# Transposed scores that accumulate key differences in PSUM, with half-height second passes side by side, in a fused attention and FP4 feed-forward kernel

## What is computed

```python
x = x + attn(layernorm(x))          # B, N, DIM = 4, 1024, 128
x = x + ffn(layernorm(x))           # hidden width 352

def attn(x):
    q, k, v = heads(x @ Wq.T), heads(x @ Wk.T), heads(x @ Wv.T)
    sim = einsum('bhid,bhjd->bhij', q, k) * 64 ** -0.5
    m = max(sim, axis=-1, keepdims=True)
    e = exp(sim - m)
    attn = e / (sum(e, axis=-1, keepdims=True) + 1e-10)
    return merge(einsum('bhij,bhjd->bhid', attn, v)) @ Wo.T + bo

def ffn(x):                          # every operand through fp4_quant_dequant first
    gate, y = fp4_linear(x, w_gate), fp4_linear(x, w_up)
    return fp4_linear(silu(gate) * y, w_down)
```

## Time and profile before

| | |
|---|---|
| median of 3 runs | 1536.1 us (1535.93 to 1537.97) |
| the profiled execution: its time | 1537.8 us |
| its span in the trace | 1535.9 us |
| TensorE busy | 1465.5 us, 95% of the span |
| GpSimd busy | 1247.4 us, 81% |
| ScalarE busy | 1162.8 us, 76% |
| VectorE busy | 1090.2 us, 71% |
| TensorE's share of the chain that ended last | 81% |
| mean granted TensorE clock | 0.985 of 2.4 GHz |

### The profile page before, as it was taken

The page is one execution under the profiler, slowest core; times in us unless marked ns, Lnnn a source line. Parts: engine busy times, 40 slices in busy tenths (PEclk is TensorE's granted clock), DMA queues, the critical chain, the costliest instruction groups (busy, mean ns, idle before and its releaser), DMA issues.

```text
span 1535.9 us, 35256 instructions
## 1 busy us (share of the span) xinstructions
PE 1465.5 (95%) x13828; PEld 971.5 (63%) x13828; DVE 1090.2 (71%) x1717; ACT 1162.8 (76%) x2413; POOL 1247.4 (81%) x1391
## 2 busy tenths in 40 slices
PE   4999999999999999999999999999999999999965
PEld 2566666666666666666666666666666666666644
DVE  7666676677667777686776767677676767767567
ACT  3788888877777777777777778777777877777832
POOL 4888989888888888787888878788888888878942
PEclk8999999999999999999999999999999999999987
DMA  6111110101111111111110111111111111111000
GB/s 166 43 42 43 43 42 22 42 23 43 43 42 43 32 35 27 43 43 46 43 26 23 46 43 42 46 28 37 25 46 43 43 43 25 26 42 46 1 4 14
DMA packets 46660, 59.77 MB, mean 39 GB/s; under 512 B 8672, under 2 KB 21920, under 8 KB 46496
## 3 DMA queue, kind: packets, MB, share of 16 engines
q1 hardware_dynamic: 46336, 57.26, 15.9%
q10 hardware_dynamic: 160, 0.26, 0.1%
HBM read 4.80 MB, written 2.10 MB: 4 GB/s over the span
## 4 chain that ended last, share of the span: by engine, by line
PE 81%; DVE 11%; ACT 4%; issue 2%; POOL 1%; DMA 1%; SPq 0%; DVEq 0%
PE ob L633 26%; PE st L605 15%; PE st L607 12%; PE sm L586 10%; PE mb L522 5%; PE mb L538 4%; DVE negm L939 3%; PE mb L527 2%; PE mb L1239 2%; PE mb L533 1%; ACT probs L759 1%; POOL p_low L449 1%; PE mb L1250 1%; PE mb L551 1%; DVE qv L1110 1%
## 5 line engine op out<-in xcount | busy, mean ns | idle before, releaser
L449 POOL TENSOR_TENSOR p_low<-probs 128x512 f16<-128x512 f32 x1024 | 1086.2, 1073 | 226.1 <-ACT probs L759 219.2
L759 ACT ACTIVATE probs<-st,lift,exp_scale 128x512 f32<-128x512 f32 x1024 | 793.4, 775 | 199.9 <-PE st L607 181.1
L939 DVE TENSOR_REDUCE negm<-sm 128x1 f32<-128x1024 f32 x508 | 617.9, 1216 | 162.6 <-PE sm L586 161.2
L605 PE MATMUL st<-q_hl,k_hh 128*128 128x512 f16 x1024 | 393.8, 385 | 2.3 <-DMA q_hm<-m_low 2.3
L607 PE MATMUL st<-q_hm,k_l 128*128 128x512 f16 x1024 | 388.5, 379 | 0.0
L633 PEld LDWEIGHTS ob<-v,p_low 128*128 128x128 f16 x4096 | 275.2, 97 | 123.0 <-POOL p_low L449 3.3
L633 PEld LDWEIGHTS ob<-v,probs 128*128 128x128 bf16 x4096 | 276.1, 98 | 120.7 <-ACT probs L759 0.5
L633 PE MATMUL ob<-v,p_low 128*128 128x129 f16 x4096 | 316.6, 219 | 2.5 <-POOL p_low L449 2.4
L633 PE MATMUL ob<-v,probs 128*128 128x129 f16 x4096 | 317.5, 220 | 0.2
L586 PE MATMUL sm<-k_hh,q_hl 64*128 64x512 f16 x508 | 197.1, 388 | 17.7 <-DVE negm L939 17.7
L586 PE MATMUL sm<-k_hh,q_hm 64*128 64x512 f16 x508 | 197.3, 388 | 0.0
(11 more groups left out here) (175 smaller groups left out, 1539.4 us busy)
## 6 DMA issues: line engine op xcount, KB each, us to landing
k_hh<-k_high SPq DMA_DIRECT2D x128, 128.0 KB, 2.3
k_l<-k_low SPq DMA_DIRECT2D x64, 128.0 KB, 2.3
q_hl<-q_high SPq DMA_DIRECT2D x64, 128.0 KB, 2.3
q_hl<-q_low SPq DMA_DIRECT2D x64, 128.0 KB, 2.4
q_hm<-q_high SPq DMA_DIRECT2D x62, 128.0 KB, 2.3
x<-x SPq DMA_DIRECT2D x4, 512.0 KB, 7.2
q_hm<-m_high SPq DMA_DIRECT2D x128, 1.0 KB
q_hm<-m_low SPq DMA_DIRECT2D x128, 1.0 KB
```

The source lines that it names most:

```text
L449: return pool.tensor_tensor(p_low[b][:, j, :], p, p.bitcast(BF16)[:, 1::2], ALU.subtract)
L605: pe.matmul(st[s % 2][:, :], k_hh[n][:, s * P:(s + 1) * P], q_hl[n][:, half * HALF:(half + 1) * HALF], start=True, stop=False)
L759: nc.scalar.activation(probs[k % 2][:, s, :], st[s % 2][:, :], ACT.Exp, bias=lift[:, 0:1], scale=exp_scale[:, head, pair:pair + 1]).then_i ...
L939: nc.vector.tensor_reduce(negm[k % 2][:, s // 2:s // 2 + 1], banks[:, :, :].rearrange("p a n -> p (a n)"), AX.X, ALU.max, negate=True).the ...
```

## The change

Keys are replaced by differences. Block s of the keys from s = 2 on holds key block s minus key block s - 2, and the bank `st[s % 2]` is never cleared inside a unit: it adds the difference's scores to the scores of block s - 2. Therefore:

- the row maximum is only added in slots 0 and 1 (`low_and_max`); from slot 2 on the second pass has only the low part of the keys, 64 rows, and those of slots s and s + 1 run as two 64-row matmuls one behind the other, in the two halves of the array, in the even slot (`low_pair`). They wait for the exponential of slot s - 1, since they write both banks;
- the maxima need the keys themselves, so a new job y0, y1 makes them (one pass of 512 columns each, high parts only), ACT takes them to `y_parts`, and SP copies them to `k_y`. The jobs k0 and k1 now multiply by the transposed differences of x (`xTd`), and move from (0, 1) and (0, 3) to (2, 3) and (2, 5); POOL makes the differences of x once per batch, and jobs E0, E1 (round 0), e0, e1 (rounds 3, 5, 7) transpose them;
- `scores` and the maxima of DVE move from the odd to the even slots; `scores` stands between the first pass and `low_pair`;
- v0 moves to bank 1 and (2, 7), v1 to bank 0 and (3, 5);
- SP copies y in the place of k, and k (ten copies instead of six) behind the store and ahead of `place_max(3)`;
- ACT's `sums` move from slots 1 and 5 to 0 and 4, `scaled` from behind the exponential of slots 2 and 6 to ahead of it; DVE's reciprocal for bank 1 from slot 1 to ahead of the maximum of slot 0;
- the exponential's bias is the number 8.0 instead of a tile.

```diff
-        ("q0", 0, (0, 5), (0, 6), (0, 6)), ("t0", 0, (0, 7), (1, 0), None), ...
+JOBS = [("y0", 0, (0, 1), (0, 2), None), ("m", 1, (0, 1), (0, 2), (0, 2)), ("y1", 1, (0, 3), (0, 4), None),
...
             in round_ of SyncE
+                    wait(sp, s_y, 2 * g + 2)
                     for h in range(2):
+                        for c in range(2):
+                            sp.dma_start(k_y[n + h][c * DH:(c + 1) * DH, :],
+                                         y_parts[h * DH:(h + 1) * DH, c * HALF:(c + 1) * HALF]).then_inc(s_dy[h], 16)
...
                 if ffn_two(r, 2) is not None:
                     ffn.store(sp, out_t, s_out, x2, ffn_two(r, 2))
                 if nxt:
+                    wait(sp, s_hi, 4 * g + 4)
+                    for h in range(2):
+                        high = k_parts[0][h * DH:(h + 1) * DH, :]
+                        sp.dma_start(k_hh[n + h][0:DH, :], high).then_inc(s_dkh[h], 16)
+                        sp.dma_start(k_hh[n + h][DH:P, :], high).then_inc(s_dkh[h], 16)
+                    wait(sp, s_lo, 4 * g + 4)
+                    for h in range(2):
+                        low = k_parts[1][h * DH:(h + 1) * DH, :]
+                        sp.dma_start(k_l[n + h][DH:P, 0:2 * P], low[:, 0:2 * P]).then_inc(s_dkl[h], 16)
+                        pairs = low[:, 2 * P:N].rearrange("d (t two j) -> d two t j", two=2, j=P)
+                        for two in range(2):
+                            sp.dma_start(k_l[n + h][two * DH:(two + 1) * DH, 2 * P:].rearrange("d (t j) -> d t j", j=P),
+                                         pairs[:, two, :, :]).then_inc(s_dkl[h], 16)
                     place_max(3)
...
             in round_ of TensorE
+                    def low_pair(n, s):
+                        wait(pe, s_ex, 32 * (g - 1) + 8 * k + s)
+                        cols = slice(P + s // 2 * P, 2 * P + s // 2 * P)
+                        for two, q_rows in enumerate((q_hl[n], q_hm[n])):
+                            rows = slice(two * DH, (two + 1) * DH)
+                            last = pe.matmul(st[two][:, :], k_l[n][rows, cols], q_rows[rows, half * HALF:(half + 1) * HALF],
+                                             start=False, stop=(two == 0), skip_group_check=True)
+                            if two == 0:
+                                last.then_inc(s_st, 1)
...
-                        if has_max and s % 2:
+                        if cur and s < 2:
+                            first_pass(n, s, True)
+                            low_and_max(n, s).then_inc(s_st, 1)
+                        elif cur and s % 2:
+                            first_pass(n, s, False).then_inc(s_st, 1)
+                        elif cur:
+                            first_pass(n, s, False)
+                        if has_max and s % 2 == 0:
                             scores(s)
+                        if cur and s >= 2 and s % 2 == 0:
+                            low_pair(n, s)
...
             in round_ of ScalarE
-                            nc.scalar.activation(probs[k % 2][:, s, :], st[s % 2][:, :], ACT.Exp, bias=lift[:, 0:1],
+                            nc.scalar.activation(probs[k % 2][:, s, :], st[s % 2][:, :], ACT.Exp, bias=SCALE * LIFT,
...
             in round_ of VectorE
-                        if has_max and s % 2:
-                            wait(dve, s_sm, 8 * (unit + 2) + s + 1)
+                        if s == 0 and (prev if k < 2 else cur):
+                            reciprocals(g, q, k, 1)
+                        if has_max and s % 2 == 0:
+                            wait(dve, s_sm, 8 * (unit + 2) + s + 2)
```

More of the change, by code:

```diff
@@ L104, in runs @@
     name = JOBS[n][0][0]
-    if name in "qkv":
+    if name in "yqkv":
         return nxt
+    if name == "E":
+        return r == 0
+    if name == "e":
+        return 3 <= r <= 2 * B - 1 and r % 2 == 1
     if name in "to":
@@ L158, in build @@
         xn = sb("xn", [P, TB, DIM])
+        xnd = sb("xnd", [P, TB - 2, DIM])
+        xTd = [sb(f"xTd_{part}", [P, B, N - 2 * P], F16) for part in ("high", "low")]
         bo_b = sb("bo_b", [P, DIM])
@@ L237, in build @@
         s_xe = sem("xT_low_made")
+        s_xd = sem("xn_differences_made")
+        s_y = sem("y_made")
+        s_dy = [sem(f"y_placed{h}") for h in range(2)]
         s_hi = sem("hi_made")
@@ L405, in bias, with differences @@
                                    bo_b[:, :].unsqueeze(1).to_broadcast([P, TB, DIM]), ALU.add).then_inc(s_bo, 1)
+            def differences(b):
+                pool.wait_ge(s_xn, 4 * (b + 1))
+                wait(pool, s_xe, 4 * b)
+                pool.tensor_tensor(xnd[:, :, :], xn[:, 2:TB, :], xn[:, 0:TB - 2, :], ALU.subtract).then_inc(s_xd, 1)
             root(0)
@@ L414, in _ @@
             scale_w(1, 4, 8).then_inc(s_ws[1], 1)
+            differences(0)
             pool.wait_ge(s_vs, 9)
@@ L442, in round_ @@
                             root((r + 1) // 2)
+                        if 3 <= r < 2 * B and r % 2 and (k, s) == (0, SLOTS - 1):
+                            differences(r // 2)
                         if 3 <= r < 2 * B and r % 2 and (k, s) == (3, SLOTS - 1):
@@ L470, in turn_x, with turn_differences @@
                     last = pe.transpose(bank[:, t * P:(t + 1) * P], xn[:, 4 * c + t, :], ident[:, :])
+                return last
+            def turn_differences(bank, b, c):
+                pe.wait_ge(s_xd, b + 1)
+                for t in range(2 + 2 * c):
+                    last = pe.transpose(bank[:, t * P:(t + 1) * P], xnd[:, 2 * c + t, :], ident[:, :])
                 return last
@@ L570, in scores @@
                         h = n % 2
-                        if k % 2 == 0 and s == 1:
-                            wait(pe, s_dkh[h], 32 * (g + (1 if k else 0)))
+                        if k % 2 == 0 and s == 0:
+                            wait(pe, s_dy[h], 32 * (g + (1 if k else 0)))
                             wait(pe, s_dqh[h], 32 * (g + (1 if k else 0)))
@@ L677, in take @@
                 ready = job_ready(g, r, m)
-                if name[0] == "q":
+                if name[0] == "y":
+                    if g == 0:
+                        act.wait_ge(s_ks, 8)
+                    wait(act, mb_ready[JOBS[m][1]], ready)
+                    for h in range(2 * (1 - c)):
+                        wait(act, s_dy[h], 32 * g)
+                    nc.scalar.activation(y_parts[:, cols], bank[:, :], ACT.Copy,
+                                         scale=k_scale[:, g % PAIRS:g % PAIRS + 1]).then_inc(s_y, 1)
+                elif name[0] == "q":
                     wait(act, mb_ready[JOBS[m][1]], ready)
@@ L700, in take @@
                     high_x(r // 2, c, bank)
+                elif name[0] in "eE":
+                    wait(act, mb_ready[JOBS[m][1]], ready)
+                    n = (2 + 2 * c) * P
+                    nc.scalar.activation(xTd[0][:, r // 2, 2 * P * c:2 * P * c + n], bank[:, 0:n], ACT.Copy).then_inc(s_xh, 1)
                 elif name[0] == "w":
```

122 lines of the change are left out of this document (71 added, 51 removed), and 16 rows, old and new, of the table JOBS.

## The result

The changed kernel takes **1652.5 us** (median of 4 runs, 1651.3 to 1655.7) against 1537.0 for the kernel before on the same chip: ratio 1.075, 95% interval 1.074 to 1.077. The direction was forecast, the size was not: 1608 us was the prediction and 1642 the upper end of the range. 44 us were missing from the sum.

What follows compares the result with a forecast made beforehand. TensorE's stream was taken as the bound, every new wait paid in full. Terms -65 + 49 + 10 + 36 + 17 + 23 + 3 + 3 = +76, less 4 for overlap, on 1536.1 gave 1608 us; range 1550 to 1642.

Steps and rivals of the forecast that it cites:

- PE's work: TensorE's stream: half-height pairs cut two slots from 2.20 to 1.99 us; with added passes and transposes, -65 us.
- rival 4: A pair's weights can't be loaded during the pair before: +38 us, 1646 us; chance 0.05.
- Bank waits: PE's jobs wait for banks because DVE's takes stand behind the maximum, mostly 0.62 us each: +49, +10 and +36 us.
- Nothing: Odd feed-forward rounds: h1 waits 0.2 us behind m, t0 waits 0.2 less, so no added time.
- The exponential: At (0, 5) and (3, 3) the lift delays the exponential: PE waits 0.7 and 0.75 us, eleven or twelve rounds, +17.
- SP's queue: Odd feed-forward rounds: k's ten copies behind the store delay m_low's copy; next unit 0 waits 2.1 us, eleven times, +23.
- 4 us off for waits that cover each other: Taken off the sum because closely following waits, such as the lift's and the queue's in one unit, partly cover each other.
- DVE's 16 us "stay": PE's old waits of 16 us for DVE's maximum come from its quantisation steps and stay, in another slot.
- rival 3: ACT becomes the second bound: the exponential keeps 0.775 us and takes push it, 30 us more, 1638 us; chance 0.13.

Runs made afterwards that it cites:

- everything ahead: Changed kernel with VectorE's takes, reciprocal of bank 0 and all quantisation steps issued ahead of the row maximum of their slot: 1545.5 us.
- the lifts late: Changed kernel with takes ahead of the maximum and every feed-forward lift one slot later on ScalarE: 1568.3 us; with the store last too, 1569.6 us.

## Why the prediction went wrong

| kernel | us | against the one above |
|---|---|---|
| changed | 1652.5 | |
| + takes ahead | 1586.5 | -66 |
| + reciprocal ahead | 1556.3 | -30 |
| + 'and' ahead | 1529.4 | -27 |
| + store last | 1521.0 | -8 |

- **PE's work (-65):** right as a price. Two slots take 1.99, as forecast, the second pair 0.22 behind the first. That busy time fell by 13 us only is no argument against it: each of the 176 recorded waits from 100 to 1560 us hides 0.16 us in the record ahead of it, and in the fastest kernel, with fewer waits, busy time is 49 us under before. Rounds 2, 4 and 6, where no feed-forward work stands, are 42.43 us with everything ahead against 43.25 before, still with waits in them. That rival 4 is wrong needs no experiment: in 348 of 378 slot pairs the low pair starts 0.22 behind scores, and of the others 25 wait for an exponential. The Trainium skill's rule (TensorE: Matmul & The Clock Gate, Part 3) that a weight load overlaps with matmuls in flight only where its row group differs does not describe this trace. The same part also lets a load for the background weight buffer go ahead, which would allow what the trace shows.
- **Bank waits (49 + 10 + 36 = +95):** right in kind and place: L596 and L616 have their waits at 0.5 to 1.3 us. Putting the takes ahead removed 66, while waits for the maximum came in. For the odd rounds, however, I wrote that only h1 is new, "Nothing". That step failed. I had followed which take stands behind a maximum, and not what stands ahead of the maximum. Three quantisation steps did, and y1 waited 1.68 us where I had 0.2, eleven times: 16 us as recorded, 18 from start to start.
- **The exponential (+17):** the mechanism is the one described, a lift that waits for a DVE step behind a maximum. The size was wrong, since I gave that step its old duration. It took 1.20 us on the mean (704 wide) where it took 0.53, and 0.95 (256 wide) where it took 0.27, because it now began with a GpSimd instruction, nearly always p_low, under way. PE waited 26 times 1.2 us, 31.6, the weights' rounds included, against 0.7 forecast. From start to start it is 1.4 each, 36 in all, so the term was short by 19. Alone, removing it is worth 1 us: the copy of m_low is due next, and the clock takes the rest.
- **The reciprocal of `den`:** absent from the sum. I had counted takes and quantisation as what a maximum holds up, and not this 0.15 us instruction. With the takes ahead it is worth 30 us. It is no part of the 44 that were missing as far as the trace shows: in the changed kernel ScalarE waits for it, but all of PE's waits for the exponential are at the lifts, and they fall to 0.2 us with the reciprocal still behind the maximum.
- **SP's queue (+23):** right: 16.0 us in eleven recorded waits, and 20 us when the store was moved. In the other kernels it is worth from 0 to 8.
- **The weights' rounds:** I had no term for rounds 5, 7 and 8. They gave 11 us, of which four waits of a low pair and two stretches at half clock (in 7 and 8) are part.
- **PE's clock:** no term either. Before, the clock stays at its full level from 60 us to the last S^T pass; now it falls three times in that part, some 1.5 us each, an estimate from round 14 (unit 0 of 12.23 us against 10.73).
- **4 us off for waits that cover each other:** no run shows it as a term of this size. Between terms the overlap is larger than that: the 'and' is worth 27 last and 1 first.
- **DVE's 16 us "stay":** no: 6.2 in the changed kernel, 10 in the other direction.
- **Together:** y1 18, the low pair 19, the clock 5 and the 4 us taken off are 46; the queue (5 less than forecast) and DVE's old waits (10 less) bring it to 31 of the 44. The other 13 lie in smaller waits that I can't part.
- **Rivals:** the number of rival 4 (1646) came closest and that of rival 3 (1638) next, both by luck. The second pair's 0.22 us refutes the mechanism of rival 4. The exponential takes 0.687 us and not the 0.775 of rival 3, and even at 0.775 the kernel is only 4.4 us slower.

What stays open: how the 66 us divide among the single takes, by which waits the even rounds rise when the store goes last with the lifts late, and what holds rounds 5, 7 and 8 (46.8, 48.8 and 47.3 us in the fastest kernel against 45.0, 46.2 and 44.0 before). Two stretches at half clock, in 7 and 8, are a part of the last; the change also moves w1, a transpose of weights, from (2, 7) to (3, 1) in round 7, and no run parts that.

## What to carry to other kernels

When an instruction moves to another slot on an engine that works in order, list everything that then stands behind it and ahead of it, down to the 0.15 us reciprocals, and who waits for each. An engine that is busy 67 to 71% of the span, as VectorE here, can still set the pace through that list. Order that work by who waits for it: takes, reciprocals and what another engine's step needs go ahead of a reduction whose consumer is a slot away; that, with the store behind the copies, turned this change from 7.5% slower into 1.1% faster. Prices of single waits are not terms of a sum: each is worth what the next-latest event leaves. Where a saving makes another wait longer, look at the clock behind that wait too.

## What the runs showed of the hardware

**VectorE and GpSimd hold each other up, and mostly by start order.** The 'and' on 704 columns takes 0.52 us when GpSimd is idle at its start; begun while a GpSimd instruction has some time left, it takes that rest and 0.38 more: rest 0.28 of an `o_n`, 0.66 us; rest 0.87 of a p_low, 1.25; rest 1.00, 1.38. At 256 columns it is 0.27 us alone and the rest and 0.15 more (rest 0.80, 0.95; rest 0.87, 1.02). In the changed kernel all 24 of these steps began so, 23 with a p_low and one with an `o_n` under way. The groups of the changed kernel:

```profile
L1206 DVE TENSOR_SCALAR qw<-qv 128x704 uint32<-128x704 uint32 x12 | 14.4, 1204 | 0.0
...
L1206 DVE TENSOR_SCALAR qw<-qv 128x256 uint32<-128x256 uint32 x12 | 11.4, 953 | 0.0
```

In the fastest kernel the 256 wide steps are at 0.28 and the 704 wide at 0.49, and there recorded starts do not decide:

```profile
575.26 0.14 DVE L1034 RECIPROCAL rden<-den 128x2 f32<-128x2 f32 x1
575.34 0.49 DVE L1212 TENSOR_SCALAR qw<-qv 128x704 uint32<-128x704 uint32 x1
...
575.28 1.45 POOL L488 TENSOR_TENSOR p_low<-probs 128x512 f16<-128x512 f32 x1
```

p_low is recorded 0.05 us ahead of the step, as in the slow case above, yet it is p_low that takes 1.45 instead of 1.04. A reciprocal of VectorE begins 0.02 ahead of both; no run tells whether that is the reason.

A duration read before a change can double by being moved 50 ns, and a cheaper instruction elsewhere (the exponential, 0.09 us shorter) can cost 7 us.

**PE's clock after waits of some 2 us.** In the changed kernel the granted clock is 1.00 from 650.6 to 651.9, behind the wait of 2.14 us, 0.52 from 651.9 to 655.3, and 0.98 after that (the third number from the end of the row):

```profile
651.90:655.30 3.40, 3.40 (x21) 1.56 (x18) 1.43 (x2) 2.07 (x6) 2.08 (x2) 0.52 0.00 0
```

0.52 is about the lower of its two levels, 1.2 GHz, while PE was busy again. The wait of 2.15 us two rounds earlier, and those of 1.2 to 1.6 us in later rounds, have no such stretch behind them. With the 'and' alone ahead, seven of the eleven waits for the copy (2.1 to 3.2 us) have one and four have none, so the length of the wait alone doesn't tell which. Each cost 1.5 us or more: unit 0 of the next round takes 12.2 to 13.4 us instead of 10.72.
